# One transformer stack on one core: the first head's maxima made ready inside part one, the sums of the weight signs moved into the heads

## The reference, cut to what matters

```python
# layer 0, attention part (16 heads of 16)
ca = _mha(input_tensor, ctx_tensor, mask, cq_w, ..., cv_b)      # over 77 context rows
x  = _self_output(ca, input_tensor, co_w, co_b, co_g, co_be)    # product, residual, layer norm
sa = _mha(x, x, None, sq_w, sq_b, sk_w, sk_b, sv_w, sv_b)       # self attention, 1024 x 1024 a head
x  = _self_output(sa, x, so_w, ...)
inter = gelu(x @ fi_w + fi_b); x = _self_output(inter, x, fo_w, ...)
# layer 0, mixture of 8 experts, top 2;  layer 1, attention with 10 prefix rows
# layer 1, feed-forward with ternary weights
scale = clip(mean(abs(w_latent), axis=1), 1e-05)                # one scale a row
tern  = clip(round(w_latent / scale), -1, 1)                    # sign by the threshold scale/2
h = x @ (tern_fc * scale_fc).T + gate * (x @ v.T @ fast_b.T @ u.T)
out = square(relu(h)) @ (tern_proj * scale_proj).T
```

## Time and profile before

| | us |
|---|---|
| median of 3 runs | 1131.09 (1127.72 to 1136.28) |
| the profiled execution's own time | 1130.95 |
| its span | 1129.2 |
| PE busy in the span | 1021.5 (90%) |
| DVE, ACT, POOL busy | 785.3, 610.2, 330.5 |
| granted clock of TensorE, mean | 0.958 |

### The profile page before, as it was taken

The page is one execution under the profiler, slowest core; times in us unless marked ns, Lnnn a source line. Parts: engine busy times, 40 slices in busy tenths (PEclk is TensorE's granted clock), DMA queues, the critical chain, the costliest instruction groups (busy, mean ns, idle before and its releaser), DMA issues.

```text
span 1129.2 us, 20786 instructions
## 1 busy us (share of the span) xinstructions
PE 1021.5 (90%) x7648; PEld 603.3 (53%) x7648; DVE 785.3 (70%) x1337; ACT 610.2 (54%) x1191; POOL 330.5 (29%) x724
## 2 busy tenths in 40 slices
PE   4899979939999999999997998949899999999997
PEld 2675656413333333333334656626687776576764
DVE  5686676528999999999924547543645677887575
ACT  2575645337888888888873122202233456656543
POOL 4422010021221222222213325362285544421010
PEclk9999999859999999999998988969899999999999
DMA  7302122242122122122117010020254411100000
GB/s 206 64 15 90 44 83 101 103 150 62 46 72 76 46 69 76 46 71 72 37 32 244 6 33 19 10 84 10 62 176 134 122 53 45 33 29 1 20 10 29
DMA packets 97746, 75.68 MB, mean 67 GB/s; under 512 B 49890, under 2 KB 87663, under 8 KB 97391
## 3 DMA queue, kind: packets, MB, share of 16 engines
q1 hardware_dynamic: 94575, 65.96, 19.6%
q0 software_dynamic: 3072, 8.39, 2.3%
HBM read 42.94 MB, written 30.93 MB: 65 GB/s over the span
## 4 chain that ended last, share of the span: by engine, by line
PE 67%; DVE 10%; DMA 8%; SPq 4%; ACT 4%; issue 3%; POOL 3%; DVEq 0%; POOLq 0%; ACTq 0%
PE TR L843 16%; PE OUT L843 14%; PE OUT L1073 10%; PE TR L849 8%; PE TR L1062 8%; DMA head_q<-MT 5%; PE OUT L1062 4%; SPq L644 3%; PE TR L919 2%; PE SCR L903 2%; SPq L732 2%; DVE small L1459 1%; ACT PTS L1283 1%; PE SCR L896 1%; POOL dispatched L2004 1%
## 5 line engine op out<-in xcount | busy, mean ns | idle before, releaser
L1528 DVE TENSOR_REDUCE small<-SCR 128x1 f32<-128x1024 f32 x256 | 308.7, 1223 | 35.1 <-PE SCR L950 29.1
L1373 ACT ACTIVATE shared<-TR 128x512 f32<-128x512 f32 x321 | 184.9, 597 | 39.9 <-PE TR L1062 33.8
L950 PE MATMUL SCR<-head_k,head_q 48*128 48x512 f32 x512 | 196.2, 461 | 5.2 <-issue 5.2
L1073 PE MATMUL OUT<-shared,HM 128*32 128x256 f32 x2048 | 166.7, 397 | 1.3 <-ACT shared L1373 0.4
L1062 PE MATMUL TR<-head_q,head_k 51*128 51x512 f32 x321 | 135.0, 453 | 18.5 <-DMA head_q<-MT 18.3
L1887 POOL TENSOR_SCALAR small<-small 128x1 f32<-128x1 f32 x112 | 27.8, 248 | 368.0 <-DVE small L1460 366.0
L1373 ACT ACTIVATE shared<-OUT 128x512 f32<-128x512 f32 x191 | 114.2, 598 | 22.6 <-PE OUT L1062 18.2
L843 PE MATMUL TR<-xT,fifo 128*128 128x512 f32 x224 | 108.6, 643 | 1.5 <-ACT xT L1261 1.5
L1062 PEld LDWEIGHTS TR<-head_q,head_k 51*128 51x128 f32 x321 | 55.6, 188 | 82.8 <-issue 31.0
L1073 PEld LDWEIGHTS OUT<-shared,HM 128*32 128x32 f32 x2048 | 41.5, 108 | 94.2 <-ACT shared L1373 56.4
L1283 ACT ACTIVATE PTS<-TR 96x512 f32<-96x512 f32 x128 | 69.8, 589 | 39.3 <-PE TR L849 38.8
(11 more groups left out here) (235 smaller groups left out, 1888.4 us busy)
## 6 DMA issues: line engine op xcount, KB each, us to landing
pieces<-pieces SPq DMA_DIRECT2D x16, 512.0 KB, 2.9
HM<-dispatched SPq DMA_DIRECT2D x46, 128.0 KB
expert_out<-HM SPq DMA_DIRECT2D x46, 128.0 KB
dispatched<-HB SPq DMA_DIRECT2D x6, 768.0 KB, 4.0
head_q<-pieces SPq DMA_DIRECT2D x32, 128.0 KB
head_k<-pieces SPq DMA_DIRECT2D x32, 128.0 KB
shared<-in_L_ffn_w SPq DMA_DIRECT2D x4, 1024.0 KB, 10.6
x<-TOK SPq DMA_DIRECT2D x16, 128.0 KB, 1.7
```

The source lines that it names most:

```text
L950: ins = nc.tensor.matmul(SQ[kt % 2][:, hf, :], QX[n % 2][rows, kt * 128:(kt + 1) * 128], KX[n % 2][rows, hf * 512:(hf + 1) * 512], start=T ...
L1073: ins = nc.tensor.matmul(PV[32 * g:32 * g + 32, 0:256], VH[:, n % 2, kt, :], PTB[:, kt % 2, g * 256:(g + 1) * 256], start=(kt == 0), stop= ...
L1373: nc.scalar.activation(PTB[:, kt % 2, hf * 512:(hf + 1) * 512], ring_bank("t_scores", n, kt, hf), ACT.Exp, scale=DH ** -0.5).then_inc(st_d ...
L1528: nc.vector.tensor_reduce(nm[:, n % 2, kt:kt + 1], SQ[kt % 2].rearrange("p h n -> p (h n)"), AX, ALU.max, negate=True).then_inc(sq_done.se ...
```

## The change

1. A new step MT in part a. The split of both first heads' maxima is done by POOL at MX.0.7 and MX.1.7 in its walk; MT transposes head 0's (PE), copies them (ACT) and moves them (SP, three DMAs). The handoff's transpose, copy and move go, and the ring of three banks starts one item earlier.
2. SP's LH is two steps. LH.0 waits for the pieces, loads heads 0 and 1, and only then writes the ones with 4 DMAs (one of three rows each, from a tile [3, 1024] in a free part of fifo). LH.1, later, loads heads 2 and 3.
3. ACT's ten sums leave the handoff: one at kt 6 of each of heads 2 to 11.
4. DVE's four thresholds move to head 12, kt 4. POOL's signs begin with head 13: one piece of wproj a head to head 28, and a piece of wfc in every second one.
5. A signal of its own for POOL's last 23 memsets, so that constants_ready comes before the routing constants; DVE waits for it ahead of part c.
6. ORDER_A is another list. In it FL stands behind QK.3, near the end.

```diff
@@ ORDER_A, the places that are spoken of
-... S.0 KW LN0.5 LN0.4 LN0.6 RA.3 S.1 E.0 RA.5 LS.7 VV T.0 E.1 S.2 PV.0 T.1 LN0.7 ...
+... S.0 E.0 LS.7 LS.5 KW S.1 T.0 VV LS.4 E.1 PV.0 RA.2 S.2 T.1 LS.6 OT.0 GG PV.1 LN0.4 ...
-... QK.1 S.12 T.11 SV.7 RA.10 LT.8 E.12 PV.11 PN.9 CT.10 S.13 T.12 LH PJ.10 ... S.15 LT.9 CT.12 PN.11 MX.0.0 ...
+... QK.1 S.11 LH.0 QP.3 PJ.9 E.11 OT.10 S.12 T.11 SV.6 E.12 PN.8 ... S.15 CT.12 MX.0.0 LT.10 LH.1 E.15 ...
-... MX.1.2 PN.15 MX.1.3 LT.14 FL LT.15 MX.1.4 MX.1.5 QK.3 SV.12 MX.1.6 SV.14 MX.1.7 SV.15 SV.13
+... MX.1.1 ... LT.12 PN.14 MT PJ.15 ... MX.1.4 LT.15 SV.14 QK.3 MX.1.5 MX.1.6 FL MX.1.7 SV.15
@@ SP
+                    for n in (2 * i, 2 * i + 1):
                         load_head(n)
+                    if i == 0:
+                        for r, g in itertools.product(range(2), range(0, 128, 64)):
+                            sp.dma_start(KX[r][g + QROWS:g + QROWS + 3, :].bitcast(F32), ones_rows[:, :]).then_inc(d_ones, 16)
+                def first_maxima_rows():
+                    sp.wait_ge(tr_done.sem, tl.after(tr_done, "MT"))
+                    store_maxima(0)
...
-                move_maxima(0)
@@ PE
+            def first_maxima_transpose():
+                pe.wait_ge(m_split.sem, 1)
+                nc.tensor.transpose(tr_bank(tl).bitcast(BF16)[0:24, 0:128], ms[:, 0, :], identb[:, :])\
+                    .then_inc(tr_full.sem, 1)
...
-            maxima_transpose(0)
@@ ACT
-            act.wait_ge(d_tern, 32)
-            for m in range(MF):
...
-            maxima_rows(0)
+                    if kt == 6 and 0 <= n - 2 < MF + KD:
+                        if n == 2:
+                            act.wait_ge(d_tern, 32)
+                        weight_sums(n - 2)
@@ DVE
+                    if (n, kt) == (MF + KD + 2, 4):
+                        weight_scales()
@@ POOL
-            ins.then_inc(c_ready.sem, 1)
+            ins.then_inc(routing_ready, 1)
...
+            def first_maxima(n, kt):
+                if kt == QT_PER_HEAD - 1:
+                    split(tl0, chain, n)
...
-            for j in range(2):
-                split(tl, chain, j)
...
+                i = n - (MF + KD + 3)
+                if 0 <= i < KD * MF:
+                    m, c = divmod(i, MF)
+                    ternary(tl, chain, wproj[:, m, c * 128:(c + 1) * 128], MF + m, False)
+                    if i % 2 == 0:
+                        ternary(tl, chain, wfc[:, i // 2, :], i // 2, True)
```

## The result

The changed kernel took 1101.26 us (median of 4 runs, 1100.47 to 1105.00) where the kernel before took 1129.4 (median of 4, 1121.59 to 1136.28): ratio 0.9751, 95% interval 0.9713 to 0.9789. Its profiled execution was the slowest of its four: 1105.00 us, span 1103.3, granted clock 0.964 (before: 1130.95, 1129.2, 0.958). The forecast of 1107 lies 2.0 us above the profiled execution and 5.7 above the median.

What follows compares the result with a forecast made beforehand. PE was taken to bound the heads, with a 15.12 us idle at the handoff that no engine bounds. Sum: 1130.95 - 14.9 - 7.4 - 4.5 + 0.3 + 2.5 = 1107 us, range 1097 to 1120.

Steps and rivals of the forecast that it cites:

- handoff: Part a to heads: head 1 starts at T + 14.3 (T: part a's end), not T + 33.2; net gain 14.9 us.
- ones and loads of heads: Before MX.0.0 in part a: 5.24 us of PE idle and 2.2 us of half clock go; gain 7.4 us.
- FL: End of part a: FL's half clock over 10.5 us leaves part a, as FL follows QK.3; gain 4.5 us.
- other reordering, with MT: Rest of part a: reordering 0, plus or minus 5 us; the new step MT costs 0.3 us, at most 1.
- sums and thresholds: In the heads: ACT's sums cost 2.3 us (bounds 0 and 5.3), DVE's thresholds 0.2 us.
- last maxima to fi, and the rest: Behind the heads: part c unchanged, 0 us in the sum.
- rival 1: Handoff: FL lowers the clock before the heads; head 0 takes 16.2 us, gain 16.7 not 14.9, total 1105; chance 0.23.
- Rival 2: Handoff: head 1's maxima move isn't held up; head 1 at T + 10.8, gain 22.4, total 1099.5; chance 0.10.
- Rival 4: Heads: half clock stays, 5.7 us per cold head; seven cold heads give 1143, 1% slower; chance 0.05.
- I price that wait at nothing, at most 2 us: SP's queue in part a: stores behind the early head loads, which hold SP about 5 us, cost 0, at most 2 us.
- so that QP.1 comes at the same time: Early part a: LN0.4 to LN0.7 hang on roots behind the same step KW, so QP.1 is not earlier; bounds 2 us.
- I give it nothing: Start of part a: constants_ready, at 9.4 us before, comes earlier but gains 0; bounds 2 us either way.

Runs made afterwards that it cites:

- loads_one_a_head: Changed kernel with wfc loaded at the handoff, wproj, fi and fo one each in heads 1 to 3, FL over 128 rows (112 zero): 1101.10 us, ratio 0.973.
- sums_left_out: Changed kernel with nine of ACT's ten sums in heads 2 to 11 left out: one run, 1100.86 us.
- routing_constants_first: Changed kernel with one signal for all constants again, so constants_ready comes behind the last 23 memsets: one run, 1103.09 us.
- first_move_behind_loads: Changed kernel with SP's move of head 0's maxima behind its four 1 MB loads of the handoff: 1116.55 us, ratio 0.986.
- fl_128_rows: Changed kernel with FL's four matmuls reading 128 rows of other data in place of 16: one run, 1104.91 us.
- fifo_weights_late: Changed kernel with the loads of fi and fo issued in head 3, behind head 4's move, not ahead of the heads: 1108.52 us, ratio 0.976.
- the six like kernels: Changed kernel and five follow-up kernels with its part a, but for one memset or SP's move; middle first score of head 0 at 214.6 us.
- weights_late_product_128: Changed kernel with all four 1 MB loads behind head 1's maxima move and FL over 128 rows, 112 zero: 1103.37 us, ratio 0.976.
- weights_after_second_move: Changed kernel with all four 1 MB loads issued behind the move of head 1's maxima, not at the handoff: 1110.23 us, ratio 0.981.
- the thirteen: The changed kernel and the twelve follow-up kernels; medians or single runs from 1100.86 to 1116.55 us.

## Why the prediction was right

The sign and the time came out, and so did the largest term. That the sum is so close is in part luck: the second term was over twice too large and the sums were charged for nothing, and both errors were made up by 7 us of part a at which nothing was put. In the profiled executions:

| term | predicted | measured |
|---|---|---|
| handoff | -14.9 | -15.1 |
| ones and loads of heads | -7.4 | -3.0 |
| FL | -4.5 | -3.7 |
| other reordering, with MT | +0.3 | -7.0 |
| sums and thresholds | +2.5 | -0.2 |
| last maxima to fi, and the rest | 0 | +3.2 |
| sum | -24.0 | -25.8 |

- **Handoff.** Head 1 was to start at T + 14.3 after 3.5 us of idling; it started at T + 13.9 after 1.40. The idling was shorter because head 0 was half cold (12.5 us in place of 10.5), which is rival 1 in part, and because the maxima landed 0.4 us sooner than forecast. The clock then fell all the same and cost 4.4 us (18.4 us from head 1's first score to the transpose in head 2, where 3.4 and 10.6 are taken at the full clock, by loads_one_a_head); 4.0 was taken. Two kernels with the same handoff (sums_left_out, routing_constants_first) had a colder head 0, hence no wait and no second fall, and B of 28.3 and 27.9. So rival 1 and the forecast are both real, and which occurs changes between runs; 15.1 is the poorer draw. Rival 2 (the move isn't held up) is refuted by 6.62 us and by first_move_behind_loads. Rival 4 (half clock through the heads): in no kernel did the clock fall again behind the start of head 2.
- **Ones and loads of heads.** The term was mis-sized in "the 5.24 us idle goes": 2.74 us stay, for DVE, which the step named as next late. Behind the wait, 3.4 us of work ran at half in place of 4.5, worth 0.5 where 2.2 was forecast. "I price that wait at nothing, at most 2 us" was right for the store behind LH.0, but only with four ones: with twelve the same store cost 6.6 us of PE.
- **FL.** The clock fell at 204.9 by its row and not at 204.6, so 10.2 us were at half; 2.9 us of that length still lie before the end of part a. The cause is shown by fl_128_rows and by the two other kernels with 128 rows.
- **The other reordering.** This is the step that failed: "I see no other stall over 2 us; 0, with plus or minus 5 us", and "so that QP.1 comes at the same time". The kernel before had waits of 2.31, 1.98 and 1.73 us for DVE's normalised inputs, 7.6 us in all; the new list left 2.3, and added 1.0 us of waits for DVE's work on the cross attention's scores. PE's idle time outside the start and MX.0.0 fell by 4.0 us and its busy time, the clock apart, by 0.9. PE began 2.1 us sooner (7.33 for 9.43), which "I give it nothing" left out; in routing_constants_first 2.9 us at the start went with 3.5 at the end of part a. The prefix rows were not the wall: their values were issued at 31.3 in fifo_weights_late and at 30.4 in loads_one_a_head, and QP.1 came at 47.6 and at 49.3. About 2 of the 7.0 us are scatter, by the six like kernels. For MT, PE's transpose took 0.23 us; no run isolates the rest.
- **Sums and thresholds.** The slack was read from one pair of exponentials (0.31 us a kt). ACT has such a wait at most key tiles, so a sum of 0.42 us disappears between waits of 0.52 and 0.22, and its lag is made good over the next ones.
- **Not in the sum:** +2.5 us between the last maxima and fi. The way was 39.8 to 42.4 us long in the other kernels, with no order by edit (sums_left_out 39.9, routing_constants_first 41.9). It goes with one wait of PE behind the heads, for DMA PTS<-self_out: 0.8 us before, 2.1 in the changed kernel, at most 1.4 where the way is 39.6 to 40.3 us and 1.9 to 2.3 where it is longer; in the changed kernel the clock was at half for 3.4 us behind it. What makes that DMA late stays open. The last 0.7 us lie in part c and are not explained.

## What to carry to other kernels

Two waits that end at about the same time must be removed together, and what is next in the same queue has to be looked at before either is moved: here the 4 MB went on to hold up the following head. Bulk loads are better put one by one into gaps of the queue than in a row, where their wait moves to the next consumer: the longest such wait was 0.92 us against 5.74, though the times don't prove a gain. A stall need not be long to count: of six waits of at most 2.3 us each 5.3 us went, of the one of 5.2 only 2.5. Many small DMAs ahead of a store with a two-buffer ring cost through that store, far from their own reader.

## What the runs showed of the hardware

- TensorE's clock fell with the engine busy: over four matmuls of 16 rows (at 204.9 in the kernel before), or 0.4 us behind them (at 209.7 in the changed kernel), it went from 1.00 to 0.50, and with the same matmuls over 128 rows, 112 of them zero, it stayed at 1.00 (weights_late_product_128, loads_one_a_head). The Trainium skill, page "TensorE: Matmul & The Clock Gate", section "What's actually happening", speaks of how busy the engine is; here PE was busy for 3.80 of 3.80 us over FL in the changed kernel and for 3.90 of 3.90 in fl_128_rows, and only the first lost its clock.
- How long the half clock lasts around the handoff and under the heads' matmuls (51, 48 rows, or 32 columns) is not fixed: from the restart, or from the fall where PE didn't stop, to the rise 5.4, 6.8, 8.4, 10.2, 13.7, 16.1, 17.1, 19.1 and 20.5 us were seen. It is likely one source of the scatter of several us between runs of one program.
- A wait of 1.40 us at head 1, 5 us after the clock had risen, was followed by another fall 0.2 us after its end, and sums_left_out, routing_constants_first, fifo_weights_late and weights_after_second_move, without a wait there, had no second fall; behind waits of 0.71, 0.92, 0.94 and 1.50 us in later heads there was none. That the wait caused the fall is not shown.
- SP's early issues go at another pace in each run: the first load of the prefix values was issued between 29.1 and 31.5 us in the thirteen, without any edit ahead of it.
